# Carrying 28 quads of edge-record moves between the gathers of the first layer's edge loop

## What is computed

```python
h = _layernorm(x, ln_gamma, ln_beta)
q = (h @ Wq + bq).reshape(N, H, C)
k = (h @ Wk + bk).reshape(N, H, C)
v = (h @ Wv + bv).reshape(N, H, C)
src, dst = (edge_index[0], edge_index[1])
score = jnp.einsum('ehc,ehc->eh', q[dst], k[src]) / np.sqrt(C)
m = jax.ops.segment_max(score, dst, num_segments=N)
ex = jnp.exp(score - m[dst])
denom = jax.ops.segment_sum(ex, dst, num_segments=N)
alpha = ex / denom[dst]
msg = alpha[:, :, None] * v[src]
agg = jax.ops.segment_sum(msg, dst, num_segments=N)
out = agg.reshape(N, H * C) + h @ Wskip + bskip
return x + jax.nn.relu(out)
```

## Time and profile before

| | us |
|---|---|
| median of 3 runs | 8754.21 |
| lowest, highest | 8752.72, 8754.75 |
| the profiled execution's own time | 8732.84 |
| its span | 8730.7 |

### The profile page before, as it was taken

How to read it: one execution, slowest core, us unless ns; L and a number is a source line. 1 busy time by engine, 2 the same in 40 slices (tenths; PEclk the granted TensorE clock), 3 DMA queues, 4 the chain that set the end, 5 groups by cost and what they waited for, 6 DMA issues and landing times. The chain is left out here.

```text
span 8730.7 us, 115397 instructions
## 1 busy us (share of the span) xinstructions
PE 5950.2 (68%) x29150; PEld 4463.7 (51%) x29150; DVE 5478.7 (63%) x14334; ACT 3062.8 (35%) x8921; POOL 5282.6 (61%) x5183
## 2 busy tenths in 40 slices
PE   0266887776269765555689999984477775574499
PEld 0133555554258533443467777773355553453487
DVE  8787888887666466666444444446577777435544
ACT  0111888886422210000233333322244444312322
POOL 0274666665467677777677777765677772434422
PEclk9688999998579887777699999977689986786699
DMA  9412665665156533333111111115333344563364
GB/s 305 152 53 77 172 174 172 174 174 157 41 159 204 158 99 101 102 100 102 50 27 31 27 31 29 29 20 167 110 105 104 105 101 117 162 212 87 116 202 161
DMA packets 634474, 1018.36 MB, mean 117 GB/s; under 512 B 135962, under 2 KB 437666, under 8 KB 633644
## 3 DMA queue, kind: packets, MB, share of 16 engines
q0 software_dynamic: 243360, 540.20, 23.1%
q1 hardware_dynamic: 364796, 418.40, 15.2%
q10 hardware_dynamic: 25744, 53.10, 2.0%
HBM read 793.35 MB, written 225.75 MB: 117 GB/s over the span
## 5 line engine op out<-in xcount | busy, mean ns | idle before, releaser
L4106 POOL DMA_INDIRECT gat_edges_rows<-gat_table,gat_room x1080 | 1163.0, 1077 | 338.9 <-issue 327.6
L2584 POOL DMA_INDIRECT l_edges_ring<-pairs,first_room x832 | 843.4, 1014 | 520.4 <-issue 239.5
L2146 POOL DMA_INDIRECT l_sum_rows<-l_feats,back_room x832 | 828.6, 996 | 265.3 <-issue 237.9
L2166 PE MATMUL l_sum_o<-l_sum_rows,l_sum_s 128*128 128x256 f32 x1664 | 604.0, 524 | 467.1 <-DVE l_sum_s L2177 236.3
L2635 ACT ACTIVATE l_edges_ring<-l_edges_ring,l_edges_weight 128x64 f32<-128x64 f32 x3328 | 816.6, 336 | 0.0
L2166 PEld LDWEIGHTS l_sum_o<-l_sum_rows,l_sum_s 128*128 128x128 f32 x1664 | 409.8, 260 | 654.8 <-DVE l_sum_s L2177 348.0
L2707 PE MATMUL l_edges_o<-l_edges_ring,l_edges_sf 128*128 128x260 f32 x1664 | 537.2, 429 | 128.8 <-DVE l_acc L2840 121.9
L3737 ACT ACTIVATE m_ffn_ht<-m_ffn_hp,m_ffn_b1t 128x256 f32<-128x256 f32 x592 | 280.1, 473 | 873.8 <-PE m_ffn_hp L3705 873.0
L2188 DVE TENSOR_TENSOR l_acc<-l_acc,l_sum_o 128x256 f32 x832 | 349.4, 420 | 351.9 <-PE l_sum_o L2166 260.5
L3715 PE MATMUL m_ffn_yp<-m_ffn_w2b,m_ffn_ht 128*128 128x256 f32 x2368 | 548.1, 385 | 28.5 <-ACT m_ffn_ht L3737 27.4
L3705 PE MATMUL m_ffn_hp<-m_ffn_xt,m_ffn_w1b 128*128 128x256 f32 x2368 | 548.3, 385 | 8.7 <-DVE m_ffn_xt L3752 5.1
(11 more groups left out here) (869 smaller groups left out, 14618.2 us busy)
## 6 DMA issues: line engine op xcount, KB each, us to landing
sorted_rows<-count_main_zero ACTq DMA_DIRECT2D x1, 51858.0 KB
m_ffn_xs<-sorted_rows SPq DMA_DIRECT2D x144, 258.0 KB, 3.5
m_ffn_w1b<-in_L_ffn_w SPq DMA_DIRECT2D x32, 1024.0 KB, 5.9
m_ffn_w2b<-in_L_ffn_w SPq DMA_DIRECT2D x32, 1024.0 KB, 5.1
m_ffn_w1b<-in_L_ffn_W SPq DMA_DIRECT2D x56, 512.0 KB, 4.6
m_ffn_w2b<-in_L_ffn_W SPq DMA_DIRECT2D x56, 512.0 KB
m_by_node<-gat_edges_ys SPq DMA_DIRECT2D x96, 256.0 KB
count_main_attr<-in_edge_attr SPq DMA_DIRECT2D x34, 644.0 KB
```

The lines of the kernel that those rows point to most:

```text
L2146: pool.indirect_dma_start(rows[:, slot, j, :], None, table, bass.IndirectOffsetOnAxis(ap=L.src[:, t:t + 1], axis=0)).then_inc(got[slot], 16)
L2166: pe.matmul(o[:, j, 0:D], s4[:, q % S4, j, :], rows[:, slot, j, :], start=True, stop=True).then_inc(out_done, 1)
L2584: pool.indirect_dma_start(rows(q, 0, 2 * D)[:, j, :], None, table, bass.IndirectOffsetOnAxis(ap=L.src[:, t:t + 1], axis=0)).then_inc(got[q ...
L4106: pool.indirect_dma_start(rows[:, slot, j, :], None, table, bass.IndirectOffsetOnAxis(ap=L.src[:, q * B + j:q * B + j + 1], axis=0)).then_ ...
```

## The change

`MOVES` takes 16 quads from the first experts, 6 from `l1_proj` and 6 from `gat_proj`. The 28 quads go to the edge loop of the first layer through a new class. It has four slots in a tile that lies idle then (`core.weight[3]`), which SP fills one quad at a time, waiting before a refill until the slot's scatters have landed. POOL issues a quad's four scatters behind the gathers of a quad, one such move per 7 or 8 quads. The phase has nine semaphores more (35 clears in place of 26). `RingCarrier.move` waits per quad, `Carrier` once.

```diff
-MOVES = (3, 6, 58, 8, 5, 2, 62, 27, 21, 4)
+MOVES = (3, 6, 58, 8, 5, 2, 46, 21, 15, 4, 28)
+class RingCarrier:
+    SLOTS = 4
...
+    def sync(self, sp):
+        for m in range(self.quads):
+            k, at = m % self.SLOTS, (self.first + m) * 5 * Q
+            if m >= self.SLOTS:
+                sp.wait_ge(self.stored[k], 16 * Q * (m // self.SLOTS))
+            sp.dma_start(self.rec[:, k, :], self.L.unmoved[:, at:at + 5 * Q]).then_inc(self.fetched[k], 16)
...
+    def move(self, pool, lo, hi):
+        for m in range(lo, hi):
+            k = m % self.SLOTS
+            pool.wait_ge(self.fetched[k], 16 * (m // self.SLOTS + 1))
+            pool.sem_inc(self.taken, 1)
+            for j in range(Q):
+                pool.indirect_dma_start(
+                    self.L.everywhere, bass.IndirectOffsetOnAxis(ap=self.rec[:, k, 4 * Q + j:4 * Q + j + 1], axis=0),
+                    self.rec[:, k, 4 * j:4 * j + 4], None).then_inc(self.stored[k], 16)
...
+            @block.sync
+            def _(sp):
+                carrier.sync(sp)
...
                         pool.indirect_dma_start(rows(q, 0, 2 * D)[:, j, :], None, table,
                                                 bass.IndirectOffsetOnAxis(ap=L.src[:, t:t + 1], axis=0)
                                                 ).then_inc(got[q % LANE_SETS], 16)
+                    carrier.move(pool, q * carrier.quads // n, (q + 1) * carrier.quads // n)
```

More of the change, by code:

```diff
@@ L274, in _, with __init__ @@
             self.move(pool, 0, self.quads)
-MOVES = (3, 6, 58, 8, 5, 2, 62, 27, 21, 4)
+MOVES = (3, 6, 58, 8, 5, 2, 46, 21, 15, 4, 28)
+class RingCarrier:
+    SLOTS = 4
+    def __init__(self, nc, ph, parts, room):
+        (self.L, self.first, self.quads), = parts
+        self.rec = room[:, 0:self.SLOTS * 5 * Q].bitcast(I32).rearrange("p (s k) -> p s k", s=self.SLOTS)
+        self.fetched = [ph.sem(f"records_fetched{k}") for k in range(self.SLOTS)]
+        self.stored = [ph.gathered_sem(4 + k) for k in range(self.SLOTS)]
+        self.taken = ph.sem("records_taken")
+    def sync(self, sp):
[4 more added lines that the diff above has]
+            sp.dma_start(self.rec[:, k, :], self.L.unmoved[:, at:at + 5 * Q]).then_inc(self.fetched[k], 16)
+        for k in range(self.SLOTS):
+            sp.wait_ge(self.stored[k], 16 * Q * len(range(k, self.quads, self.SLOTS)))
+    def move(self, pool, lo, hi):
[7 more added lines that the diff above has]
+                    self.rec[:, k, 4 * j:4 * j + 4], None).then_inc(self.stored[k], 16)
 class Unmoved:
@@ L2516, with edge_attend @@
 APART = float(2 ** 96)
-def edge_attend(nc, core, L, name, table, queries, acc, scale):
+def edge_attend(nc, core, L, name, table, queries, acc, scale, beside):
     H, W, n, CQ, U, BK = 4, D, L.quads, 4, 14, 2
@@ L2567, in edge_attend @@
         got = [ph.gathered_sem(k) for k in range(LANE_SETS)]
+        carrier = RingCarrier(nc, ph, beside, core.weight[3][:].rearrange("p t k -> p (t k)"))
         whole = dict(unroll=U, lead=n + 16, in_order=True)
@@ L3044, in layer0_gnn @@
     with nc.sbuf_tensor("l0_acc", [P, T, D + 4], F32) as acc:
-        edge_attend(nc, core, first, "l0_edges", pairs, core.x, acc, 0.125)
+        edge_attend(nc, core, first, "l0_edges", pairs, core.x, acc, 0.125, unmoved.take(MOVES[10]))
         finish_gnn(nc, core, "l0_finish", acc, 4, table=skip, beside=unmoved.take(MOVES[3]), park=park)
```

## The result

| | before | after |
|---|---|---|
| median of the runs, us | 8754.21 (8752.72 to 8754.75) | 8824.94 (8824.00 to 8839.87) |
| profiled execution, us | 8732.84 | 8824.94 |
| ratio of after to before | | 1.0088, 95% interval 1.007 to 1.0106 |

What follows compares the result with a forecast made beforehand. The edge loop was taken as a POOL-DVE ring without slack at a chunk's first quad. +119 there less 23 from donors gave +96: 8829 profiled, 8850 as median; own range 8825 to 8875, whole 8780 to 8890.

Steps and rivals of the forecast that it cites:

- the same difference, added here: Whole kernel: the shown runs' median lies 21.4 us above the profiled execution; adding this turned 8829 into 8850.
- The loop, +119 predicted: Edge loop: 115.5 us for moves plus 3.2 for one more long POOL gap, bounds 0 and 153.
- the moves: Edge loop: 27 groups of four scatters, 5.2 us of POOL each, less slack by place: 107.9 times 1.07, 115.5 us.
- the gaps: POOL in the edge loop: one more pause of about 3 us as its instruction stream grows, 3.2 us.
- subtracting POOL's wait and DVE's spare 0.65 us: Edge loop: 5.2 us less available slack leaves 5.2, 3.64, 3.65, 3.46 us ahead of first to fourth quad.
- the first rival: Edge loop: POOL becomes the bound, each move costs its whole 5.2 us times 1.07; +130 us, 8884; chance 0.17.
- The second rival: Edge loop: the ring wins part of the delay back, about half of 119 remains; +37 us, 8791; chance 0.13.
- The packets, 0: Edge loop: scatters' packets in the gathers' queue drain beside POOL's issue; 0 taken, 15 us upper bound.
- SP's late fetches, 0.02: Edge loop: SP's small fetches come late and hold POOL before its move; above 8900 us; chance 0.02.
- The donors, -23 predicted: Experts give 8 us, `l1_proj` 8.6 and `gat_proj` 6.6; together 23, bounds 13 and 29.
- POOL's waits for scores under 130: Sign in the edge loop's trace after: POOL's waits for DVE's scores shrink from 201.9 us to under 130.
- absorbed, and faster: Edge loop: moves fit into POOL's 201.9 us of waits, leaving only the donors' gain; 8732 us; chance 0.07.

Runs made afterwards that it cites:

- the run of the loop alone: Changed kernel's edge loop with its moves, but earlier and later carriers keep all 196 quads as in the kernel before: 8860.1 us, ratio 1.0116.
- the experiment with four at a place: Changed kernel with its 112 scatters regrouped by stretches, one stretch having four behind quad 2 of each chunk: 8804.7 us, ratio 1.0051.
- the hold without a transfer: Kernel before with POOL held by 20 iotas at each of the changed kernel's 28 places in the loop: 8885.8 us, ratio 1.0144.

## Why the prediction was right, and where it was not

**The whole.** Predicted +96 us on the profiled execution, +92.1 came. By the medians it is 71, and 8824.94 us is at the very edge, 0.06 us outside, of the forecast's own range of 8825 to 8875: the 21.4 us that I added to both are how the profiled execution of before lay under its median, and that of after lies on its own. More than half of it lay in the unchanged last stretch. The step "the same difference, added here" is what made 8829 into 8850.

**The loop, +119 predicted, +112.6 measured, and +118.1 with the donors left alone.** The sum is right and two of its terms are wrong, in opposite directions: the moves 21 us too cheap, the gaps 27 us too dear. That they nearly cancel is luck.
*The moves.* 27 x 4.28 = 115.5 us stood there. They cost 112.8 + 24 = 137 us, 5.1 each (5.2 in the run of the loop alone). A move is 5.39 us long and not 5.2, which is 5 us of it. Where the rest lies can be read from the chunks of the trace after, each taken from the last scores of one chunk to the last of the next:

| move ahead of the chunk's | chunks | mean, us | above 23.88 | predicted, with 1.07 |
|---|---|---|---|---|
| first quad | 7 | 30.85 | 7.0 | 5.6 |
| second | 4 | 28.17 | 4.3 | 3.9 |
| third | 8 | 27.96 | 4.1 | 3.9 |
| fourth | 8 | 27.45 | 3.6 | 3.7 |
| no move | 24 | 24.31 | 0.4 | 0 |

The run of the loop alone gives 30.8, 28.9, 27.9, 27.3 and 24.5. So subtracting POOL's wait and DVE's spare 0.65 us came out within 0.4 us in the chunk that holds the move (1.1 for the second quad in the other run). What failed are two steps beside it. Ahead of the first quad a move costs 7.0 us and not its length times 1.07, because PE's sums are waited for too: 10 us in seven moves. And a delay isn't over with its chunk: DVE is late, POOL waits for the late DVE, and the chunks without a move, which nearly all stand behind one with a move, are 0.4 us longer each, again 10 us. That was the first rival's argument ("POOL's waits ahead of later quads don't shrink, because DVE, being late, lets POOL go later too"), and by the whole price the runs are nearer to its 5.6 us a move than to my 4.28. With a move in every chunk, as in the experiment with four at a place, both parts fall into the same cycle, and of the 1.74 us ahead of the fourth quad only 1.0 is left. The second rival, that the ring wins part of the delay back, fell: the chunks without a move are on average not shorter than before, and the one behind a long gap of before only by 0.2 us.
*The gaps.* "One more of the long gaps comes, 3.2 us" was wrong: all seven went, worth 24 us, so that 3.2 stood where -24 belongs. I had taken them for something that grows with POOL's stream of instructions, and 208 more instructions left them where they were. The Trainium skill (Runtime: NRT & Kernel Launch, Instruction fetch mechanics) says that fetches of code are mostly hidden. I had held the gaps against that. The runs with more instructions give no ground for it: whatever the gaps are, nothing here shows a fetch.

**The packets, 0.** Not contradicted: the hold without a transfer has the same price per us to within 9 us over the loop. SP's late fetches, 0.02: no gather and no scatter in the changed kernel waited for a fetched slot.

**The donors, -23 predicted, -27.0 measured**, within the bounds of 13 and 29. `l1_proj` gave 7.4 for 8.6, `gat_proj` 7.9 for 6.6. The experts gave 11.7 for 8: the end on POOL came 5 us earlier relative to DVE (the last store ends 3.1 us behind DVE's last result, 7.8 before), and PE waited 5.3 us for its rows where it had been 8.5; some 4 us more than these two are not explained.

**What was to be seen.** DVE's waits for gathers above 130 us: yes, 162.7, with waits of mostly 3 to 5.5 us behind the moves. POOL's waits for scores under 130: no, 171.6. This row alone would have told that the slack was not being used and that the forecast's mechanism was off, though its time was not. Eight long gaps: no, none. Handing over 6 us after DVE: 5.3, yes. PE's time in the experts: 462 us before, 459 after, as said.

**The rival "absorbed, and faster"**, 0.07, was false for whole moves and true for single scatters: the deciding price was 0.85 us a move, and the four scatters of a move cost about 0.2 us together when each stands alone (6 us for 104). The rival treated the slack as a property of the loop. It belongs to places: ahead of the second and of the fourth quad there is room for about one scatter each, ahead of the third too as far as one stretch of six cycles can tell, and ahead of the first there is none.

## What to carry to other kernels

In a loop that is tied in a ring, as this one is, an engine's idle time could be filled only with pieces no longer than the wait at the place where they stand: 28 pieces of 5.4 us cost 71 us (donors' gain and lost gaps counted in) where 112 pieces of 1.35 us, with the last 32 behind the loop's final gather, gained 50. Look for the place where a delay is followed by waits of several engines (here a chunk's first quad) and keep it free. Whether work is absorbed showed in two rows together: the filled engine's waits shrink and its partner's don't grow.

## What the runs showed of the hardware

- Indirect DMAs issued in a row by POOL take nearly the same time each, whether they gather 128 rows of 2 KB or scatter 128 records of 16 bytes (median 946 and 974 ns, mean 1.01 and 1.05 us), and stand 0.30 us apart.
- POOL's regular gaps of about 3 us (seven in 832 gathers, 112 apart) stayed in place with 208 semaphore instructions or 560 iotas more. With one scatter among the 832 gathers (and the semaphores and the fetch that come with it) all of them stood 12 gathers later and were 2.23 us long; with 80 to 112 scatters spread over the loop none to six were left, all shorter. The traces show no cause.
- A stall of POOL of 3.2 us ahead of a chunk's second gather cost 3.5 us; one of 2.4 us ahead of its second quad, where POOL waited 0.91 us anyway, 0.3.
